# Layer 3 of a four-layer GNN: the self terms move from one 2048-column maximum and POOL's products into DVE's last multiply

## The reference, cut to what matters

```python
XW = X @ W
s_col = XW @ a[0, :f];  s_row = XW @ a[0, f:]
Z1  = leaky_relu(s_row[:, None] + s_col[None, :], negative_slope=0.01)
den = exp(Z1)
num = A @ den
att = where(num != 0, den / where(num != 0, num, 1.0), 0.0)
H   = A @ (att @ XW)
x   = x + H
```

## Time and profile before

| | us |
|---|---|
| median of 3 runs | 747.57 (747.55 to 747.98) |
| the profiled execution, own time | 745.52 |
| its span, first to last instruction | 743.8 |
| PE busy in the span | 616.4 (83%) |
| DVE busy | 530.7 (71%) |
| ACT busy | 238.1 (32%) |
| POOL busy | 226.9 (31%) |

### The profile page before, as it was taken

One profiled execution on the slowest core, in us unless ns is written; L12 is line 12 of the kernel. 1 busy time (PEld: TensorE's weight loads), 2 busy tenths in 40 slices (PEclk: granted clock), 3 DMA queues, 4 the chain that ended last, 5 costly groups with the idle time before them and its releaser, 6 DMA issues.

```text
span 743.8 us, 15549 instructions
## 1 busy us (share of the span) xinstructions
PE 616.4 (83%) x5771; PEld 558.4 (75%) x5771; DVE 530.7 (71%) x922; ACT 238.1 (32%) x374; POOL 226.9 (31%) x164
## 2 busy tenths in 40 slices
PE   0769789999980599598891759999999999999897
PEld 0657669999980366398891259999999999999797
DVE  4675477776728364634678559999999999999811
ACT  2635001111102222375540223333333333333363
POOL 2046031111002000244331504434434454443542
PEclk9965589999965799899995669999999999999999
DMA  7856000000000000000000000000000000000001
GB/s 249 296 218 230 2 3 2 2 0 0 0 1 0 0 1 0 1 1 1 1 1 0 1 3 2 1 3 0 0 0 0 0 0 0 0 0 1 1 15 44
DMA packets 5967, 20.07 MB, mean 27 GB/s; under 512 B 416, under 2 KB 3360, under 8 KB 3872
## 3 DMA queue, kind: packets, MB, share of 16 engines
q1 hardware_dynamic: 4944, 18.88, 7.0%
q10 hardware_dynamic: 976, 0.59, 0.3%
HBM read 18.42 MB, written 1.05 MB: 26 GB/s over the span
## 4 chain that ended last, share of the span: by engine, by line
PE 28%; DVE 21%; issue 16%; POOL 1%; DVEq 1%; ACT 1%; ACTq 0%; POOLq 0%
PE bank L1029 11%; PE bank L1155 6%; PE bank L1007 6%; DVE denc L1619 4%; DVE tc L1637 4%; DVE yc L1644 3%; DVE G L1595 2%; PE bank L1165 2%; PE bank L859 1%; DVE h L1264 1%; PE bank L1059 1%; POOL diag L437 1%; DVE stats L1218 1%; DVE pr L1513 1%; PE bank L1136 1%
## 5 line engine op out<-in xcount | busy, mean ns | idle before, releaser
L1155 PE MATMUL bank<-ATc,denc 128*128 128x128 f32 x1536 | 184.8, 278 | 12.1 <-ACT ATc L814 8.4
L1155 PEld LDWEIGHTS bank<-ATc,denc 128*128 128x128 f32 x1536 | 178.2, 194 | 13.3 <-issue 9.5
L580 POOL TENSOR_TENSOR dTc<-dTc,yc 128x512 f32<-128x512 f32 x64 | 111.8, 1746 | 162.6 <-ACT yc L808 114.5
L1029 PE MATMUL bank<-pcs,Ar 128*128 128x256 f32 x768 | 94.7, 287 | 7.0 <-DVEq L1250 3.7
L1029 PEld LDWEIGHTS bank<-pcs,Ar 128*128 128x128 f32 x768 | 93.8, 196 | 8.1 <-DVEq L1250 4.6
L806 ACT ACTIVATE yc<-bank 128x512 f32<-128x512 f32 x64 | 38.2, 597 | 159.8 <-PE bank L1155 159.8
L1619 DVE TENSOR_SCALAR denc<-cB,rc 128x2048 f32<-128x2048 f32 x48 | 85.1, 1776 | 0.2 <-DVE rc L1611 0.2
L1165 PE MATMUL bank<-XW,yc 128*128 128x128 f32 x512 | 68.1, 277 | 1.8 <-DVE yc L1644 1.8
L1007 PE MATMUL bank<-pcs,A 128*128 128x385 bf16 x256 | 44.2, 334 | 28.7 <-DVEq L1243 28.7
L1644 DVE SCALAR_TENSOR_TENSOR yc<-tc,dTc 128x512 f32<-128x512 f32 x64 | 64.6, 1029 | 0.0
L1165 PEld LDWEIGHTS bank<-XW,yc 128*128 128x128 f32 x512 | 62.7, 193 | 2.1 <-DVE yc L1644 2.1
(11 more groups left out here) (195 smaller groups left out, 852.6 us busy)
## 6 DMA issues: line engine op xcount, KB each, us to landing
a<-in_adj SPq DMA_DIRECT2D x16, 1024.0 KB, 4.8
out<-X SPq DMA_DIRECT2D x4, 256.0 KB, 2.2
W<-in_L_gnn_W ACTq DMA_DIRECT2D x1, 192.0 KB, 6.4
attB<-in_L_gnn_att_weight ACTq DMA_DIRECT2D x1, 128.0 KB, 4.7
a3B<-in_L_gnn_a ACTq DMA_DIRECT2D x1, 128.0 KB, 9.4
W<-in_L_gnn_weight ACTq DMA_DIRECT2D x1, 64.0 KB, 1.8
W<-in_L_gnn_W ACTq DMA_DIRECT2D x1, 64.0 KB, 6.8
X<-in_x SPq DMA_DIRECT2D x1, 0.5 KB, 8.6
```

The costliest lines, as they stand in the source:

```text
L580: nc.gpsimd.tensor_tensor(own, own, yc[b][c][:, :], ALU.mult).then_inc(yd_ready, 1)
L1029: last = nc.tensor.matmul(bank[t % 2][:, 0:2 * D], Ar[t % 4][:, kt, :], pieces[:, kt, :], start=kt == 0, stop=kt == T - 1)
L1155: last = nc.tensor.matmul(bank[c][:, P * k:P * k + P], denc[b][:, part, j0:j0 + P], ATc3[b][:, part, :], start=part == 0, stop=part == NC - 1)
```

## The change

The self terms are no longer stored. `own3` (16 maxima of 2048 columns in all) and POOL's `times_own` (64 products of 512 columns) go, with the semaphores `own3_ready` and `yd_ready`; `dTc` is not written any more. `refine` now forms (tc - 2) times y in `tc` itself. Behind it a new DVE function `times_own` forms max(t, q) times that, in four operations of 128 columns a chunk: the per-partition scalar q of the 128-column block is an operand, so that maximum and multiply are one instruction. `refine` and `times_own` of a chunk come straight behind its `times_y`; before, `refine` came one chunk later. POOL's list for the stage is only its last wait.

```diff
--- before.py
+++ after.py
@@ -268,8 +268,7 @@
         ln_ready = sem("ln_ready")
         y_ready = sem("y_ready")
         t_ready = sem("t_ready")
-        own3_ready = sem("own3_ready")
-        yd_ready = sem("yd_ready")
+        fine_ready = sem("fine_ready")
         att3_ready = sem("att3_ready")
         att3_used = sem("att3_used")
         un3_kept = sem("un3_kept")
@@ -572,21 +571,7 @@
                 steps(pool, lo_step, att_step)
                 pool.wait_ge(u_bank, 4)
 
-            def times_own(it, b, c):
-
-                pool.wait_ge(own3_ready, it + 1)
-                pool.wait_ge(y_ready, 4 * it + c + 1)
-                own = dTc[b][:, 4 * c:4 * c + 4, :].rearrange("p j i -> p (j i)")
-                nc.gpsimd.tensor_tensor(own, own, yc[b][c][:, :], ALU.mult).then_inc(yd_ready, 1)
-
-            def tile3(it, b):
-                times_own(it, b, 0)
-                times_own(it, b, 1)
-                times_own(it, b, 2)
-                times_own(it, b, 3)
-
             def by_slots3():
-                sweep(pool, tile3)
                 pool.wait_ge(num3_bank, 4 * (T - 1) + 8)
 
             choose(pool, 3, by_slots3, over_all3)
@@ -1619,16 +1604,6 @@
                 nc.vector.tensor_scalar(denc[b][:, c, :], qB3[:, :], rc[b][:, c, 0:1], rc[b][:, c, 1:2],
                                         ALU.mult, ALU.max).then_inc(denc_ready, 1)
 
-            def own3(it, b):
-
-                if within(it, -2):
-                    dve.wait_ge(att3_ready, 4 * it + 4)
-                if not isinstance(it, int):
-                    apart(dve)
-                nc.vector.tensor_tensor(dTc[b][:, :, :],
-                                        tB3[:, bass.ds(it * P, P)].unsqueeze(1).to_broadcast([P, T, P]),
-                                        q3.unsqueeze(2).to_broadcast([P, T, P]), ALU.max).then_inc(own3_ready, 1)
-
             def times_y(it, b, c):
 
                 n = 4 * it + c
@@ -1639,31 +1614,37 @@
             def refine(it, b, c):
 
                 n = 4 * it + c
-                dve.wait_ge(yd_ready, n + 1)
+                dve.wait_ge(y_ready, n + 1)
                 dve.wait_ge(t_ready, n + 5)
-                nc.vector.scalar_tensor_tensor(yc[b][c][:, :], tc[c % 2][:, :], 2.0,
-                                               dTc[b][:, 4 * c:4 * c + 4, :].rearrange("p j i -> p (j i)"),
-                                               ALU.subtract, ALU.mult).then_inc(att3_ready, 1)
+                nc.vector.scalar_tensor_tensor(tc[c % 2][:, :], tc[c % 2][:, :], 2.0, yc[b][c][:, :],
+                                               ALU.subtract, ALU.mult).then_inc(fine_ready, 1)
+
+            def times_own(it, b, c):
+
+                dve.wait_ge(fine_ready, 4 * it + c + 1)
+                if not isinstance(it, int):
+                    apart(dve)
+                for k in range(4):
+                    last = nc.vector.scalar_tensor_tensor(yc[b][c][:, P * k:P * k + P], tB3[:, bass.ds(it * P, P)],
+                                                          q3[:, 4 * c + k:4 * c + k + 1], tc[c % 2][:, P * k:P * k + P],
+                                                          ALU.max, ALU.mult)
+                last.then_inc(att3_ready, 1)
 
             def tile3(it, b):
                 if within(it, 2):
                     one_hot3(it + 2, b)
                 for c in range(4):
-                    if within(it, 1):
-                        if c < NC:
-                            den3(it + 1, 1 - b, c)
-                        else:
-                            own3(it + 1, 1 - b)
+                    if within(it, 1) and c < NC:
+                        den3(it + 1, 1 - b, c)
                     times_y(it, b, c)
-                    if c > 0:
-                        refine(it, b, c - 1)
+                    refine(it, b, c)
+                    times_own(it, b, c)
                     if c == 2 and within(it, 2):
                         edges3(it + 2, b)
                     if not within(it, 1) and c < NG - 1:
                         if c == 0:
                             dve.wait_ge(un3_kept, GT * (NG - 1) + 2)
                         split_wide(Un[:, group(c), :], pcs3, c)
-                refine(it, b, 3)
 
             def by_slots3():
 
@@ -1692,7 +1673,6 @@
                 dve.wait_ge(bc_copied, 56)
                 for c in range(NC):
                     den3(0, 0, c)
-                own3(0, 0)
                 edges3(1, 1)
                 sweep(dve, tile3)
                 dve.wait_ge(un3_kept, T + 2)
```

## The result

The changed kernel takes **764.97 us** (median of 4 runs, 761.18 to 765.88) against 747.56 for the kernel before on the same chip (4 runs, 746.13 to 747.98): ratio 1.0227, 95% interval 1.0189 to 1.0264. It is slower, as forecast, but by 17.4 us where 8.9 were forecast; the forecast 756.5 lies low, and the range's upper bound, 765.0, holds the median by 0.03 us. The profiled execution took 765.53 us with a span of 763.8.

The account below looks back on a forecast made before the run. DVE was taken to set the pace at 16.60 us a tile; -1.7 for the first two tiles, +7.5 for the loop and +3.1 for the last two gave 8.9 us slower, 756.5 us, range 748.5 to 765.

Parts of the forecast that it names:

- What goes: DVE's loop tile: the maximum, 2.21 us, and POOL's slowing of `denc` and `refine`, 2.7 us; together 4.9 us less.
- What comes: DVE's loop tile: 16 added operations of 128 columns at 0.259 us from start to start, 4.14 us a tile.
- The rival by which hand-overs cost nothing: DVE loses nothing waiting for its own result: 0.96 us less a tile, -6.5 us in all, 741.1 us; chance 0.09.
- The second rival, hidden increments: Increments and register work ahead of `times_own` run during `refine`: 0.54 us less a tile, 750.0 us; chance 0.08.
- The third, starved short operations: Short operations run at their whole record, 0.34 us: 1.3 us more a tile, 778 us in all; chance 0.08.
- gaps of 0.36 throughout: Range's upper end: all gaps ahead of `times_own` at 0.36 us add 0.74 a tile, 8.9 in all, giving 765.
- The lower end: Range's lower bound, 748.5 us: 1.5 under the second rival's 750.0, for the casts not meeting DVE.
- The chain inside a chunk: DVE's dependent operations: 0.12 us for each of eight hand-overs, gaps of 0.15 or 0.25 ahead of `times_own`; tile 17.22 us.
- The edges, 0.80: End of DVE's loop tile: `edges3` 0.55 us plus a gap of about 0.25, together 0.80.
- y of chunk 0 is there at 446.05, before and after: Start of tile 0: the first y arrives at an unchanged time; with shorter tiles, the first two gain 1.7 us.
- Sum 29.4 ... I add one cast's length, 1.9: Last two tiles: 29.4 us plus 1.9 for POOL's casts meeting DVE, 31.3 against 28.2 before, 3.1 us lost.
- PE's own work is 15.9: PE in a loop tile: 16.59 less 0.70 idle, so a tile can gain 0.7 us at most before PE bounds.

Follow-up runs that it names:

- experiment 5: Changed kernel with refine's second wait removed and DVE reordered so another operation stands between each producer and consumer: 738.38 us, ratio to before 0.9869.
- first profile of before: The unchanged kernel before, as first profiled: profiled execution 745.52 us, span 743.8 us, first `denc` at 436.02.
- experiment 1: Changed kernel with one wait less: `refine` no longer waits for `y_ready`; 761.33 us, ratio to before 1.0170.
- second profile of before: The kernel before, unchanged, profiled once more: 749.01 us (one run), span 747.3 us, first `denc` at 439.43.
- Experiment 3: Changed kernel with POOL's first cast behind the loop waiting until the last short operation is done: 762.71 us, ratio to before 1.0192.
- experiment 2: Changed kernel with `times_own` one chunk late, same instructions, waits and increments: 744.57 us, ratio to before 0.9960.
- experiment 4: Changed kernel with POOL's 64 products put back on data that nobody reads: 791.05 us (one run).

## Why the prediction was right or wrong

**Right: the direction and its cause.** What goes came as worked out: the maximum is gone, `denc` and `refine` fell to their undisturbed lengths, POOL is idle. What comes ate more than that, by the eight hand-overs a tile. The rival by which hand-overs cost nothing was the one to beat, and the Trainium skill states its rule (VectorE: DVE Perf Modes, The DRAIN you can't avoid). Here the measurement decides against it: experiment 5 has the same operations as the changed kernel, with nothing changed but the order and a redundant wait, and its tile is 17.53 - 15.78 = 1.75 us shorter. The second rival, hidden increments, falls by the 0.25 in chunk 0 and the 0.15 in each of the other three, exactly the gaps that the prediction had taken from the earlier trace rows. The third, starved short operations, falls by 1.06 for four.

**Luck: that the range holds the median.** Its upper end stood for gaps of 0.36 throughout (756.5 + 8.9 is 765.4 rather than 765), and the gaps came out near the forecast case, 0.15 to 0.32. What filled the range are four shortfalls, against the first profile of before: 1.7 us in the first two tiles, 3.6 in the loop, 1.9 in the last two tiles and 1.2 in the last product; only the loop's lies where the range had looked. The lower end is a little off too: it takes 1.5 for the casts, where the term is 1.9.

**Mis-sized: the loop, +7.5 forecast, +11.1 measured** (from tile 2's first operation to tile 14's: 690.42 - 480.14 = 210.28, against 199.16). By the steps of "The chain inside a chunk" and "What comes", against the tile shown: `times_y` to `refine` was 4 x 0.72 = 2.88 and is 0.73 + 0.72 + 0.79 + 0.81 = 3.05, since the step priced one wait and in chunks 2 and 3 the instruction has two (experiment 1 gave 0.15 a tile back). The short operations, 4.14, are 4.23. `refine` to the first short one, 3.42, is 3.47. The edges, 0.80, are 0.87, with a gap of 0.32 where 0.25 was taken. The rest is as forecast to 0.02. Sum 17.58, the tile's length, against 17.22: no single step failed, each was short by 0.05 to 0.17, and all on the same side.

**Wrong: the first two tiles, -1.7 forecast, 0.0 against the first profile of before, -0.75 against the second.** Two steps failed. One is "y of chunk 0 is there at 446.05, before and after": `times_y` waited 2.71 for ACT and began at 449.48, 10.73 behind the first `denc`, against 10.14 before (446.16), at a lower granted clock (0.79 in the window 440 to 460, 0.90 before). That is not the change's: in the second profile of before, at 0.83, the distance is 10.73 too (450.16 - 439.43). The other is the length of the two tiles, 13.1 and 16.6 forecast: they took 13.59 and 17.07 (to the selection matrices at 463.07 and 480.14), and the second wait of `refine` in eight chunks is some 0.6 of that 1.0.

**Mis-sized: the last two tiles, +3.1 forecast, +5.0 measured.** From tile 14's first `denc` (690.42) to the end of the last `u3` are 33.16 us, against 28.2 before; the step "Sum 29.4 ... I add one cast's length, 1.9" gave 31.3. The casts cost 2.4 instead of 1.9, the second wait 0.6, the last `u3` 2.1 instead of 1.8 at a lower clock. What was right is the mechanism: POOL's list without products reaches its casts early. Experiment 3 takes these stalls out of tile 14.

**Missed: the last product, 0 forecast, +1.2.** The prediction ended with the last `u3`. The windows view of the 11.4 us behind the last `u3`, in the changed kernel and in the second profile of before:

```profile
723.60:735.00 11.40, 9.52 (x57) 9.52 (x58) 1.12 (x2) 8.16 (x8) 2.63 (x2) 0.65 0.00 1
```

```profile
708.28:719.68 11.40, 9.51 (x67) 9.51 (x68) 1.12 (x2) 8.12 (x9) 4.31 (x3) 0.85 0.00 1
```

57 matrix instructions at a granted clock of 0.65 against 67 at 0.85, in the same 9.5 us of PE's time. PE had waited 1.71 and 2.80 us ahead of its last two `u3`; in experiment 5 it waited 0.82 and 0.62, and the stretch behind the last `u3` is 39.04 again. That suggests the waits as the cause, but other runs speak against the waits alone: in experiment 2 PE waited 0.73 and 2.46 us and the stretch is 39.03, in experiment 4 it waited 4.59 ahead of the last `u3` and the stretch is 39.29. So the lower clock is shown, and its cause stays open.

**Too high: "PE's own work is 15.9".** It changed no term of the sum, but it is why experiment 5 was expected at 15.9 or above: 15.71 is what its rows show.

## What to carry to other kernels

On an engine that runs in order, price an operation that consumes the result just ahead of it by its start to start distance in such a place, not by its length: here 0.12 us for the hand-over, 0.06 to 0.08 for a second wait, 0.1 for an increment and 0.2 with register work beside it, 1.7 us a tile in all. Before a fused or moved operation is judged, look for independent work to put between producer and consumer: the change was 2.3% slower as written and 1.3% faster in another order with one wait less. And where an engine loses work, look at what stands next in its list, and what that will run beside.

## What the runs showed of the hardware

- A wait that is long satisfied isn't free on DVE: with two on one instruction the gap to the record ahead is 0.11 (561.53 + 0.68 to 562.32), with one 0.04 (561.11 + 0.69 to 561.84).
- A POOL cast of 128 x 2048 beside DVE stretches DVE's operations: four short ones from 1.14 to 2.65 us, a split from 0.69 to 2.26. `times_y`, which reads PSUM and one SBUF tensor, keeps its 0.68 to 0.69 in all 64 places of the kernel before, where POOL was busy for 73.59 of 165.86 us. The Trainium skill names the pair (Advanced Engine Details and Errata, GPSIMD Details): POOL shares a read and a write interface with DVE, in conflict with DVE instructions in a 2-port mode or with two SBUF inputs. These rows agree. The selection matrix, also with two SBUF inputs, stayed at 2.28 beside a product; there the product was the longer one, 2.50, where the one ahead of it, at 574.79, took 1.27.
- The kernel before reached layer 3's first `denc` at 436.0 us in one profile and at 439.4 in another, with a granted clock of 0.83 and 0.72 at layer 2's first wide product. Two profiles are best compared stretch by stretch, from a row that both have.
